# Attention in a whole-network kernel: the side chains placed one link per unit, the output bias as a product, x normalised on ScalarE, and a later wait for the last key stores

## The chip, the cores and the metric

The kernel is one program on one core of a Trainium2 chip. It computes the whole two-layer network in one launch. The metric is device time in microseconds; the kernel before ran in 1357.28 us (median of three runs, 1355.54 to 1359.51).

## The reference, cut to what matters

Eight batches of 256 rows by 512 pass through a long convolution, a quantised feed-forward layer, a cross attention with 16 heads of 32, and a mixture of experts. The change lies in the cross attention. The context has 256 rows and all of them count as image rows, so the image keys and values are all there is:

```python
q = rms_norm(layer_norm(x) @ Wq + bq, gq)     # per batch: 256 x 512
k = rms_norm(context @ Wk_img + bk_img, gk_img)
v = context @ Wv_img + bv_img
x = x + softmax(q k^T / sqrt(32)) v @ Wo + bo
```

float32 accuracy is kept by splitting a factor into two bf16 parts, high and low, and adding three products of them.

## The kernel before, in words

The stages run one after the other, each between barriers of all engines. `stage_keys_values` makes the keys and values of all batches and the queries of batches 0 and 1; keys go to DRAM in stacked form (`keys_stacked`), by three DMAs for each batch. Its SyncE program ends with waits for all its stores, the last batch's too, and the barrier waits for SyncE.

`stage_attention` walks 64 units, g = 8b + u: batch b, and u one of eight pairs of heads. Every engine has its own program, a Python loop over the same `STEPS` (b, u), written out by hand; an engine does its instructions strictly in that order and waits on semaphores. In a step, TensorE does: the transposed scores of unit g (L1551, waits for the maxima rows of g), the plain scores of g+2 (L1515, waits for the reduction of g+1), the turn of the maxima of g+1 (L1524), and the values of g-2 (L1537). VectorE copies the turned maxima into the queries' spare rows (L1449), reduces the scores of g+2 (L1467), and divides the output of g-2 (L1475, L1477). GpSimd splits the maxima of g+2 in two (L1368, L1370) and makes the low part of the probabilities of g (L1376). ScalarE does the exponential (L1422) and the high part (L1426). "The ring" in what follows is turn, copy, reduction, split, turn, which closes once for each unit.

Beside the units two side chains run, in extra instructions at fixed steps. Both use the two PSUM tiles `psP`.

- The query chain of batch b+2 (b+2 from 2 to 7): at u=4 VectorE normalises x into `xn` (L1498), at u=5 TensorE turns it (L1585), at u=6 the high part (ScalarE, L1413) and the low part (VectorE, L1461) are made and half of the 48 products done (`queries`, L1563 to L1568), the rest at u=7. At u=0 of the next batch ScalarE squares the last parts, GpSimd folds the squares (`fold_halves`, L915, L917), TensorE sums them (L908), VectorE makes v (L1482), GpSimd r = v^-1/2 (L1373); at u=1 ScalarE spreads r on diagonals (L1397), TensorE turns that into a row (L1594), VectorE scales the queries (four of L1486); at u=2 they are split (L1404, L1471) and from u=3 SyncE stacks them by 12 DMAs (L1336), which the plain scores of the batch after wait for.
- The output chain of batch b-1: at u=2 TensorE turns the output (L1601), at u=3 ScalarE and VectorE split it (L1408, L1455), and at u=3 and u=4 TensorE projects one tile each with 12 products (L893). VectorE adds the result to x (L1443) and takes statistics (L1492). The bias was added to x by GpSimd (`bias`, L1346).

So a step may hold a whole chain of four engines, with TensorE in the middle and at the end of it. At (0, 2) VectorE also clears the spare rows of the second key buffer (L1435, L1437).

## Time and profile before

| what | us |
|---|---|
| median of three runs | 1357.28 |
| profiled execution | 1357.12 |
| its span, first to last instruction | 1355.4 |
| attention stage, first instruction to the next stage's first | 593.1 to 890.8 |
| TensorE busy over the span | 1093.0 (81%) |
| VectorE / ScalarE / GpSimd busy | 930.0 / 712.1 / 618.7 |

A profile row of the windows view gives each engine's busy time in a stretch, with the count of its instructions in brackets, and then the granted TensorE clock as a share of 2.4 GHz (0.50 is 1.2 GHz). Matmuls overlap, so the time one takes on TensorE is read from the distance of two starts, and not from its duration.

### The profile page before, as it was taken

How to read it: one execution, taken by the hardware profiler on the slowest of the kernel's cores; microseconds unless marked ns; L12 is line 12 of the kernel's file. 1: busy time of each engine (PE TensorE's matmuls, PEld its weight loads, DVE VectorE, ACT ScalarE, POOL GpSimd, SP SyncE). 2: the span in 40 equal slices, each digit the busy share in tenths (PEclk: the TensorE clock that was granted, in tenths of full speed). 3: DMA queues.
4: the chain of work that ended last, by engine and by line, in shares of the span. 5: the costliest groups of instructions: out<-in, count | busy, mean ns of one | idle time of the engine just before them, and what ended most of it. 6: DMA issues, size and time to landing. Idle time of an engine off the chain costs nothing. (4 is left out here: it accounts for less than half of the span.)

```text
span 1355.4 us, 25553 instructions
## 1 busy us (share of the span) xinstructions
PE 1093.0 (81%) x9603; PEld 807.8 (60%) x9603; DVE 930.0 (69%) x1672; ACT 712.1 (53%) x1087; POOL 618.7 (46%) x580
## 2 busy tenths in 40 slices
PE   4899996369996699837888878788989879999950
PEld 4677775135553466515666655568756568888840
DVE  6489998858886676547787877678855545555526
ACT  4566755168885455425666666556424424454430
POOL 1444434224553222237776776630565335555520
PEclk9899998789999799858998998765989989999985
DMA  6574411003333313220111111067567747887749
GB/s 252 183 239 120 158 47 40 31 32 125 116 101 114 112 60 95 66 68 25 48 48 48 41 32 47 2 230 289 143 196 222 236 132 266 300 278 242 234 147 365
DMA packets 79291, 187.38 MB, mean 138 GB/s; under 512 B 10302, under 2 KB 12500, under 8 KB 78280
## 3 DMA queue, kind: packets, MB, share of 16 engines
q1 hardware_dynamic: 60040, 137.03, 30.3%
q0 software_dynamic: 8544, 24.68, 6.0%
q10 hardware_dynamic: 10592, 24.12, 5.7%
q8 instruction: 74, 1.21, 0.4%
q14 instruction: 41, 0.34, 0.1%
HBM read 131.37 MB, written 48.14 MB: 132 GB/s over the span
## 5 line engine op out<-in xcount | busy, mean ns | idle before, releaser
L376 PE MATMUL ps_y<-kv,toep 128*128 128x288 f32 x640 | 157.9, 409 | 6.9 <-DMA toep<-taps_padded 6.8
L376 PEld LDWEIGHTS ps_y<-kv,toep 128*128 128x128 f32 x640 | 122.0, 191 | 42.3 <-DMA toep<-taps_padded 8.3
L1376 POOL TENSOR_TENSOR at_pl<-at_pf,at_ph 128x1024 bf16<-128x1024 f32 x64 | 136.5, 2133 | 0.5 <-ACT at_ph L1426 0.5
L360 POOL TENSOR_TENSOR kv<-kx 128x1024 f32<-128x1024 f32 x32 | 60.6, 1894 | 88.9 <-PE ps_y L376 37.5
L1422 ACT ACTIVATE at_pf<-ps_st 128x1024 f32<-128x1024 f32 x64 | 65.3, 1020 | 59.2 <-PE ps_st L1551 55.1
L2205 POOL DMA_INDIRECT expert_results<-sgu,target x47 | 70.0, 1489 | 55.9 <-ACT sgu L2237 55.9
L1467 DVE TENSOR_REDUCE at_negmax<-ps_s 128x4 f32<-128x1024 f32 x64 | 78.2, 1222 | 14.4 <-PE ps_s L1515 12.8
L893 PEld LDWEIGHTS ps_eg<-e_xT,e_w 128*128 128x128 bf16 x1128 | 69.0, 100 | 14.3 <-DVE e_w L2278 1.9
L893 PE MATMUL ps_eg<-e_xT,e_w 128*128 128x128 bf16 x1128 | 73.1, 223 | 3.4 <-DVE e_xT L2285 3.4
L834 PE MATMUL ps_fH<-w1T,f_qaT 128*128 128x512 bf16 x256 | 64.6, 410 | 9.1 <-ACT f_h L742 8.4
L2278 DVE COPY e_w<-expert_weights 128x4096 bf16 x47 | 57.7, 1227 | 20.7 <-issue 20.7
L893 PE MATMUL ps_eu<-e_xT,e_w 128*128 128x128 bf16 x1128 | 71.2, 220 | 0.0
L1449 DVE COPY qs<-ps_m 32x256 bf16<-32x256 bf16 x128 | 37.6, 294 | 48.8 <-PE ps_m L1524 46.2
L1426 ACT ACTIVATE at_ph<-at_pf 128x1024 bf16<-128x1024 f32 x64 | 67.6, 1057 | 2.0
L2200 POOL DMA_INDIRECT sgu<-token_rows,token x45 | 44.4, 986 | 48.3 <-PE ps_ex L2327 48.3
L2291 DVE SCALAR_TENSOR_TENSOR e_y<-ps_eu,e_bias,e_y 128x128 f32<-128x128 f32 x94 | 28.7, 346 | 54.0 <-PE ps_eu L893 53.2
L893 PEld LDWEIGHTS ps_eu<-e_xT,e_w 128*128 128x128 bf16 x1128 | 65.6, 98 | 0.0
L1927 POOL TENSOR_TENSOR expert_weights<-s_raw,expert_weights 128x1024 bf16<-128x1024 f32 x16 | 37.6, 2351 | 53.3 <-ACT expert_weights L2084 53.2
L2253 ACT ACTIVATE e_xT<-ps_ex 128x512 bf16<-128x512 bf16 x47 | 28.1, 597 | 61.9 <-PE ps_ex L2327 61.9
L400 DVE TENSOR_TENSOR prod<-ps_y,qx 128x1024 f32<-128x1024 f32 x32 | 39.1, 1223 | 30.3 <-ACT ps_y L329 30.2
L859 PE MATMUL ps_fY<-w2T,f_qbT 128*128 128x512 bf16 x256 | 57.9, 379 | 0.8 <-DVE x_res L704 0.8
L2084 ACT ACTIVATE expert_weights<-s_raw 128x1024 bf16<-128x1024 f32 x32 | 33.7, 1054 | 45.7 <-DMA s_raw<-in_L_ffn_rg 34.6
(385 smaller groups left out, 3216.0 us busy)
## 6 DMA issues: line engine op xcount, KB each, us to landing
sgu<-down_parts SPq DMA_DIRECT2D x47, 512.0 KB, 4.8
w_raw<-in_L_ffn_w ACTq DMA_DIRECT2D x32, 512.0 KB, 5.1
toep<-taps_padded SPq DMA_DIRECT2D x32, 256.0 KB, 3.6
f_draw<-in_L_ffn_rw SPq DMA_DIRECT2D x16, 512.0 KB, 4.2
down_parts<-f_dparts SPq DMA_DIRECT2D x16, 512.0 KB, 2.9
s_raw<-in_L_ffn_rg SPq DMA_DIRECT2D x16, 512.0 KB, 4.4
s_raw<-in_L_ffn_rw SPq DMA_DIRECT2D x16, 512.0 KB, 5.4
m_got<-expert_results SPq DMA_DIRECT2D x16, 512.0 KB, 10.1
```

What stands on the lines that cost most here:

```text
L360: pool.tensor_tensor(pairs[:, :, :, 0:HD0], x[:, :, 0:HD0].unsqueeze(2).broadcast_to([P, ROWS_N, WIDE, HD0]), partners(x, 0, 1, WIDE), ALU ...
L376: last = pe.matmul(y[:, l * B:(l + 1) * B, :, WIDE - 1:], toep[h % 2][:, (DC - 1 - l + m) * P:(DC - l + m) * P], kv[h % 2][:, m * B:(m + 1 ...
L834: pe.matmul(psH[:, f, :], qaT[p][:, c, :], k.w1T[:, c * FF + f * 512:c * FF + (f + 1) * 512], start=(c == 0), stop=False)
L859: last = pe.matmul(psY[:, :], qbT[p][:, c, :], k.w2T[:, c * D:(c + 1) * D], start=(c == 0), stop=(c == FC - 1))
L893: instruction = pe.matmul(out, stationary[a], moving[b], start=first and n == 0, stop=last and n == 2)
L1376: pool.tensor_tensor(pl[u % 4][:, :, :, :], pf[u % 2][:, :, :, :], ph[u % 4][:, :, :, :], ALU.subtract) .then_inc(p_low, 1)
L1422: act.activation(pf[u % 2][:, :, :, :], psT[:, :, :, :], ACT.Exp, scale=SCORE_SCALE).then_inc(exped, 1)
L1426: act.activation(ph[u % 4][:, :, :, :], pf[u % 2][:, :, :, :], ACT.Copy).then_inc(p_high, 1)
L1467: dve.tensor_reduce(negmax[u % 2][:, :].rearrange("p (j q) -> p j q", j=2), psS[:, :, :, :], AX.X, ALU.max, negate=True).then_inc(max_read, 1)
L2200: pool.indirect_dma_start(out=rows[j % 2], out_offset=None, in_=k.scratch["rows"], in_offset=bass.IndirectOffsetOnAxis(ap=token[:, j:j + 1 ...
L2205: pool.indirect_dma_start(out=k.scratch["results"], out_offset=bass.IndirectOffsetOnAxis(ap=target[:, j:j + 1], axis=0), in_=yo[j % 2], in ...
L2278: dve.tensor_copy(w1[j % 2][:, :, :, :].rearrange("p h c f -> p (h c f)"), W[:, bass.ds(e, 1), :, :, :].rearrange("p o h c f -> p (o h c f ...
```

## The change

The two side chains are laid out anew, so that a step holds one link of a chain and the next link comes in a later step.

- Query chain of b+2: x is normalised by ScalarE at u=1 (`x_shift` = -mean*rstd as bias, rstd as scale); TensorE turns tile 0 at u=2 and tile 1 at u=3; products at u=4, 5, 6 (16 each); the eight square sums are eight products straight from the squares at u=7 (no fold), into the bank of the maxima (`psV`); VectorE's v and GpSimd's r and diagonals follow at u=7; TensorE's row and VectorE's scaling at u=0 of the next batch; the high part on ScalarE and the low part on GpSimd at u=2.
- Output chain of batch c: turned at (c+1, 7), split at the step after (ScalarE) and at the end of the same step (VectorE), projected in four halves at (c+2, 0) to (c+2, 3). For c=6 it is turned at (7, 4) and projected at (7, 5) and (7, 6); c=7 stays where it was.
- The output bias is the first product of each projected tile: a 33-row bf16 tile holds its high part in row 0 and its low part in row 32, against ones.
- The second wait of SyncE for the last batch's three key stores moves from the end of `stage_keys_values` to the load of batch 7's keys; the split keys' buffers live until then. The loads of keys and the stacking stand one or two steps earlier in SyncE's program.

```diff
+        self.last_stored = ctx.enter_context(nc.semaphore("last_keys_stored"))
...
+                done = k.last_stored if i == N - 1 else stacked[p]
...
-                sp.wait_ge(stacked[p], stores(N - 2 + p))
+                sp.wait_ge(stacked[p], stores(N - 2 - p))
...
+        bo = sb("at_bo", [LO_ROW + 1, D], F32)
+        bo_parts, ones_b = (sb(f"at_{n}", [LO_ROW + 1, w], BF16) for n, w in (("bop", D), ("oneb", P)))
+        x_shift = sb("at_xshift", [P, NT], F32)
...
+        maxes_and_sums = ctx.enter_context(nc.psum_tensor("ps_m", [P, D], F32))
+        psM = maxes_and_sums[:, 0:P].bitcast(BF16).rearrange("p (q t) -> p q t", q=2)
+        psV = maxes_and_sums[:, 2 * P:2 * P + TPB]
...
+        def turn_step(c):
+            return (c + 1, 7) if c < B - 2 else (B - 1, 4) if c == B - 2 else (B, 2)
+        def project_step(c, t, h):
+            return (c + 2, 2 * t + h) if c < B - 2 else (B - 1, 5 + t) if c == B - 2 else (B, 3 + t)
+        def following(step):
+            return step[0] + (step[1] + 1) // G, (step[1] + 1) % G
...
+            sp.wait_ge(bias_zeroed, 1)
+            for row in (0, LO_ROW):
+                sp.dma_start(bo[row:row + 1, :], k.ins["L1_xattn_bo"].rearrange("(o d) -> o d", o=1)).then_inc(b_loaded, 16)
...
-                if u == 2 and 0 < q < B:
+                if u == 0 and 0 < q < B:
                     if q >= 2:
                         sp.wait_ge(st_psum, (q - 1) * G)
-                    sp.dma_start(kb[q % 2][0:STACK, :, :, :], ks[q:q + 1, :, :, :, :].rearrange("o p h c s -> (o p) h c s"))                      .then_inc(k_loaded, 16)
-                if u == 3 and queried(q):
+                    if q == B - 1:
+                        sp.wait_ge(k.last_stored, KEY_INCS)
+                    sp.dma_start(kb[q % 2][0:STACK, :, :, :], ks[q:q + 1, :, :, :, :].rearrange("o p h c s -> (o p) h c s"))\
+                      .then_inc(k_loaded, 16)
+                if u == 2 and queried(q):
...
+            pool.memset(bo[:, :], 0.0).then_inc(bias_zeroed, 1)
+            pool.memset(ones_b[:, :], 1.0)
...
-                if b == 0 and u < AHEAD * TPB:
-                    pool.wait_ge(b_loaded, 16)
-                    bias(u)
-                if u == 5 and queried(b + 2):
-                    for t in range(TPB):
-                        pool.wait_ge(xn_ready, nth(b + 2) * TPB + t + 1)
-                        bias((b + 2) * TPB + t)
-                if u == 0 and queried(b + 1):
-                    q = nth(b + 1)
-                    pool.wait_ge(squared, (q + 1) * 2 * DC)
-                    fold_halves(pool, folded, 2 * q + 2, sq)
...
+                if u == 7 and queried(b + 2):
+                    n = nth(b + 2)
+                    pool.wait_ge(var_ready, n + 1)
+                    if n:
+                        pool.wait_ge(r_psum, n)
                     pool.tensor_tensor(r[:, :], v[:, :], k.pow_half[:, 0:TPB], ALU.pow).then_inc(r_ready, 1)
+                    pool.wait_ge(r_ready, n + 1)
+                    for t in range(TPB):
+                        last = pool.tensor_tensor(diag[:, t, :], k.ident[:, :], r[:, t:t + 1].broadcast_to([P, P]), ALU.mult)
+                    last.then_inc(diag_ready, 1)
...
+                if u == 2 and queried(b + 1):
+                    pool.wait_ge(q_high, nth(b + 1) + 1)
+                    pool.tensor_tensor(q_lo[:, :, :], qn[:, :, :], q_hi[:, :, :], ALU.subtract).then_inc(q_low, 1)
...
+                    act.wait_ge(q_low, q)
...
+                for c in range(B):
+                    if (b, u) == following(turn_step(c)):
+                        for t in range(TPB):
+                            act.wait_ge(ot_psum, c * TPB + t + 1)
+                            act.activation(o_hi[:, :, t * P:(t + 1) * P], psP[t][:, :].rearrange("p (c t) -> p c t", c=DC),
+                                           ACT.Copy).then_inc(ot_high, 1)
+                if u == 1 and queried(b + 2):
+                    act.wait_ge(shift_ready, 1)
                     for t in range(TPB):
...
+                        tile = (b + 2) * TPB + t
+                        act.activation(xn[t][:, :], xtile(tile), ACT.Identity, bias=x_shift[:, tile:tile + 1],
+                                       scale=x_rstd[:, tile:tile + 1]).then_inc(xn_ready, 1)
...
+                if u in (3, 4) and queried(b + 2):
+                    x_highs(nth(b + 2), u - 3)
+                if u in (5, 6) and queried(b + 2):
+                    biased_and_squared(nth(b + 2), u - 5)
                 if u == 7 and queried(b + 2):
...
+                    biased_and_squared(nth(b + 2), 2)
+                    biased_and_squared(nth(b + 2), 3)
...
+            dve.scalar_tensor_tensor(x_shift[:, :], x_mean[:, :], -1.0, x_rstd[:, :], ALU.mult, ALU.mult).then_inc(shift_ready, 1)
...
+                    lo_row = slice(LO_ROW, LO_ROW + 1)
+                    dve.wait_ge(b_loaded, 32)
+                    dve.tensor_copy(bo_parts[:, :], bo[:, :]).then_inc(bias_high, 1)
+                    dve.wait_ge(bias_high, 1)
+                    dve.tensor_tensor(bo_parts[lo_row, :], bo[lo_row, :], bo_parts[lo_row, :], ALU.subtract).then_inc(bias_low, 1)
...
+                if u == 7 and queried(b + 2):
+                    dve.wait_ge(sum_psum, nth(b + 2) + 1)
+                    dve.tensor_scalar(v[:, :], psV, 1.0 / D, RMS_EPS, ALU.mult, ALU.add).then_inc(var_ready, 1)
                 if u == 0 and queried(b + 1):
...
                     dve.wait_ge(r_psum, nth(b + 1) + 1)
                     for c in range(DC):
                         dve.scalar_tensor_tensor(qn[:, c, :], qn[:, c, :], vectors[:, ROWS["gq"] + c:ROWS["gq"] + c + 1],
...
+                                                 psP[1][:, 0:S], ALU.mult, ALU.mult).then_inc(normed, 1)
+                for c in range(B):
+                    if (b, u) == turn_step(c):
+                        out_lows(c)
                     for t in range(TPB):
...
+                        if (b, u) == following(project_step(c, t, 1)):
+                            statistics(c * TPB + t)
+                        if (b, u) == project_step(c, t, 1):
+                            added(c * TPB + t)
+                if u in (2, 3) and queried(b + 2):
+                    x_lows(nth(b + 2), u - 2)
...
+                if u == 1 and queried(b + 1):
+                    pe.wait_ge(var_ready, nth(b + 1) + 1)
...
+            def turn_x(b, q, t):
+                pe.wait_ge(xn_ready, q * TPB + t + 1)
+                if t:
                     pe.wait_ge(x_low, q * TPB + 1)
...
+                elif b >= 2:
+                    pe.wait_ge(y_added, (b - 2) * TPB + 1)
+                for c in range(DC):
+                    last = pe.transpose(psP[0][:, c * P:(c + 1) * P], xn[t][:, c * P:(c + 1) * P], k.ident[:, :])
+                last.then_inc(xt_psum, 1)
+            def query_highs(c, chunks):
+                cols = slice(c * P, (c + 1) * P)
+                for kc in chunks:
+                    pe.matmul(psP[c % 2][:, 0:S], qw[:, 0, kc, cols], x_hi[:, kc, :], start=(kc == 0), stop=False)
+                    pe.matmul(psP[c % 2][:, 0:S], qw[:, 1, kc, cols], x_hi[:, kc, :], start=False, stop=False)
+            def query_lows(c):
                 cols = slice(c * P, (c + 1) * P)
                 for kc in range(DC):
...
+                    last = pe.matmul(psP[c % 2][:, 0:S], qw[:, 0, kc, cols], x_lo[:, kc, :], start=False, stop=(kc == DC - 1))
                 last.then_inc(q_psum, 1)
+            def query_sums(g, q):
+                pe.wait_ge(squared, (q + 1) * 2 * DC)
+                pe.wait_ge(maxT_ready, 2 * (g + 2))
+                for t in range(TPB):
+                    for c in range(DC):
+                        last = pe.matmul(psV[:, t:t + 1], sq[:, c, t * P:(t + 1) * P], k.ones[:, 0:1], start=(c == 0), stop=(c == DC - 1))
+                last.then_inc(sum_psum, 1)
+            def spread(b, q):
+                pe.wait_ge(diag_ready, q + 1)
+                if b >= 2:
+                    pe.wait_ge(ot_low, (b - 1) * TPB)
+                pe.matmul(psP[1][:, 0:S], k.ones[:, :], diag[:, :, :].rearrange("p t q -> p (t q)"), start=True, stop=True)\
+                  .then_inc(r_psum, 1)
+            def turn_out(c):
+                pe.wait_ge(o_read, (c + 1) * G)
+                if c:
+                    pe.wait_ge(y_added, c * TPB)
+                if queried(c + 3):
+                    pe.wait_ge(squared, (nth(c + 3) + 1) * 2 * DC)
+                for t in range(TPB):
+                    for d in range(DC):
+                        last = pe.transpose(psP[t][:, d * P:(d + 1) * P], o[c % 2][:, t, d * P:(d + 1) * P], k.ident[:, :])
+                    last.then_inc(ot_psum, 1)
+            def project(c, t, h):
+                if h == 0:
+                    pe.wait_ge(ot_low, c * TPB + t + 1)
+                    if c == 0:
+                        pe.wait_ge(bias_low, 1)
+                    if t and queried(c + 3):
+                        pe.wait_ge(normed, (nth(c + 3) + 1) * DC)
+                    pe.matmul(psP[t][:, :], ones_b[:, :], bo_parts[:, :], start=True, stop=False)
+                for d in (2 * h, 2 * h + 1):
+                    last = three_products(pe, psP[t][:, :], [a[:, d, t * P:(t + 1) * P] for a in (o_hi, o_lo)],
+                                          [ow[:, s, d, :] for s in range(2)], False, d == DC - 1)
+                if h:
+                    last.then_inc(y_psum, 1)
             for b, u in STEPS:
                 g = b * G + u
...
                     scores(g + 2)
                 if unit(g + 1):
                     turn_maxes(g + 1)
...
                 if unit(g - 2):
                     values(g - 2)
+                if u in (2, 3) and queried(b + 2):
+                    turn_x(b, nth(b + 2), u - 2)
+                for c in range(B):
+                    if (b, u) == turn_step(c):
+                        turn_out(c)
+                    for t in range(TPB):
+                        for h in range(2):
+                            if (b, u) == project_step(c, t, h):
+                                project(c, t, h)
                 if u == 0 and queried(b + 1):
...
+                    spread(b, nth(b + 1))
+                if u == 4 and queried(b + 2):
+                    q = nth(b + 2)
+                    pe.wait_ge(x_low, q * TPB + 2)
+                    query_highs(0, range(DC))
+                    query_lows(0)
+                    if b >= 2:
+                        pe.wait_ge(y_added, (b - 1) * TPB)
+                    elif q:
+                        pe.wait_ge(normed, q * DC)
+                    query_highs(1, range(2))
+                if u == 5 and queried(b + 2):
+                    query_highs(1, range(2, DC))
+                    query_lows(1)
+                    pe.wait_ge(squared, nth(b + 2) * 2 * DC + 2)
+                    query_highs(2, range(DC))
                 if u == 6 and queried(b + 2):
...
+                    query_lows(2)
+                    pe.wait_ge(squared, nth(b + 2) * 2 * DC + 4)
+                    query_highs(3, range(DC))
+                    query_lows(3)
                 if u == 7 and queried(b + 2):
...
+                    query_sums(g, nth(b + 2))
```

## Rows read from the trace of the kernel before

**Rows 1.** Windows by batch: length, busy PE, PEld, DVE, ACT, POOL, clock, DMA share, GB/s

```profile
593.10:598.50 5.40, 3.32 (x14) 1.43 (x14) 2.86 (x4) 1.28 (x1) 0.99 (x4) 0.50 0.67 174
598.50:636.10 37.60, 25.79 (x287) 18.83 (x287) 26.20 (x43) 20.88 (x27) 27.39 (x32) 0.72 0.09 25
636.10:671.50 35.40, 28.94 (x368) 22.39 (x367) 27.63 (x56) 23.23 (x32) 26.30 (x30) 0.95 0.18 47
671.50:817.40 145.90, 119.15 (x1467) 90.71 (x1465) 110.56 (x224) 93.07 (x125) 105.08 (x117) 0.93 0.18 45
817.40:848.40 31.00, 24.30 (x307) 16.66 (x305) 23.68 (x50) 18.93 (x22) 21.59 (x25) 0.89 0.11 27
848.40:873.40 25.00, 21.47 (x268) 15.15 (x269) 18.47 (x43) 15.65 (x16) 17.59 (x22) 0.84 0.01 2
873.40:890.80 17.40, 11.77 (x104) 6.55 (x104) 5.57 (x12) 3.27 (x4) 4.09 (x2) 0.65 0.00 1
```

**Rows 2.** Waits of TensorE in the attention: total us, times, longest

```profile
PE ps_p L908 <- POOL at_sq L917: 11.0, 6, 1.8
...
PE ps_p L893 <- DVE at_olo L1455: 6.3, 8, 0.8
PE ps_p L1563 <- DVE at_xlo L1461: 6.0, 6, 1.0
PE ps_st L1551 <- ACT at_pf L1422: 5.8, 7, 0.9
```

**Rows 3.** Timeline of TensorE, one step: start, us, line and product

```profile
702.90 0.60 PE L1551 MATMUL ps_st<-qs,kb 128*128 128x256 bf16 x4
...
703.89 0.20 PE L1537 MATMUL ps_o<-v_hi,at_ph 128*128 128x33 bf16 x2
...
704.49 0.27 PE L1563 MATMUL ps_p<-at_xhi,qw 128*128 128x256 bf16 x1
...
707.11 0.60 PE L1551 MATMUL ps_st<-qs,at_kb 128*128 128x256 bf16 x4
```

**Rows 4.** Timeline of TensorE: the square sums of one batch and what follows

```profile
638.74 0.60 PE L908 MATMUL ps_p<-ones,at_sq 128*128 128x1 f32 x4 [1.84 <-POOL at_sq L917]
639.21 0.60 PE L1551 MATMUL ps_st<-qs,at_kb 128*128 128x256 bf16 x4
```

**Rows 5.** Timeline of TensorE: the projection of one tile and what follows

```profile
727.74 0.59 PE L893 MATMUL ps_p<-ow,at_ohi 128*128 128x512 bf16 x2
...
730.33 0.60 PE L1551 MATMUL ps_st<-qs,at_kb 128*128 128x256 bf16 x4
```

**Rows 6.** Timeline of GpSimd, two units with little beside them

```profile
846.18 2.13 POOL L1376 TENSOR_TENSOR at_pl<-at_pf,at_ph 128x1024 bf16<-128x1024 f32 x1
...
849.02 2.13 POOL L1376 TENSOR_TENSOR at_pl<-at_pf,at_ph 128x1024 bf16<-128x1024 f32 x1
```

**Rows 7.** One line, the normalising of x: ns least/median/most, first and last start

```profile
L1498 DVE TENSOR_SCALAR at_xn<-x_res,x_mean,x_rstd x12: 532/1268/2344, 620.6 to 804.1; 128x512 f32<-128x512 f32 x12
```

**Rows 8.** Timeline of all engines around the stage's start

```profile
582.47 0.62 SPq L1003 DMA_DIRECT2D keys_stacked<-kv_khi  x1
...
593.15 1.01 PE L1515 MATMUL ps_s<-kb,qs 96*128 96x256 bf16 x4 [16.08 <-PEq L931]
```

**Rows 9.** Waits of SyncE's queue around the stage's start

```profile
SPq L1040 <- DMA keys_stacked<-kv_khi: 9.5, 1, 9.5
```

**Rows 10.** Groups of instructions in the attention: busy us, mean ns

```profile
L1346 POOL TENSOR_TENSOR x_res<-x_res,at_bo 128x512 f32<-128x512 f32 x16 | 21.4, 1352 | 1.8 <-DVE at_xn L1498 1.8
...
L1601 PE MATMUL ps_p<-ident,at_o 128*128 128x128 f32 x64 | 10.3, 314 | 2.5 <-DVE at_qn L1486 1.9 <-DVE at_o L1477 0.6
L1486 DVE SCALAR_TENSOR_TENSOR at_qn<-at_qn,vectors,ps_p 128x256 f32<-128x256 f32 x24 | 9.9, 473 | 0.0
...
L1471 DVE TENSOR_TENSOR at_qlo<-at_qn,at_qhi 128x1024 bf16<-128x1024 f32 x6 | 7.3, 1216 | 0.0
...
L1594 PE MATMUL ps_p<-at_diag,ones 128*128 128x256 f32 x12 | 6.7, 659 | 0.1
```

More of the change, by code:

```diff
@@ L1613, in _ @@
                 if u == 7 and queried(b + 2):
-                    queries(nth(b + 2), 2)
-                    queries(nth(b + 2), 3)
+                    query_sums(g, nth(b + 2))
 E_N = 16
@@ L2445, in build @@
                 kb = left(attention, "kb0", [P, HC, DC, S], BF16)
+                k_hi, k_lo = ([left(attention, f"kv_{n}{i}", [P, DC, S], BF16) for i in range(2)] for n in ("khi", "klo"))
                 with ExitStack() as kv:
```

148 lines of the change are left out of this document (33 added, 115 removed).

## The prediction

> **What bounds the kernel now.** I read the windows by batch first. From 598.5 us to 873.4 us the 64 units take 274.9 us, and in the four middle batches (145.9 us, 36.5 each) TensorE is busy 119.15, so 29.8 of 36.5; VectorE 27.6, GpSimd 26.3, ScalarE 23.3 [rows 1]. No engine is full. Then the waits of TensorE: 11.0 us in six times for the folded squares, 6.3 for the low part of the output, 6.0 for the low part of x, 5.8 for the exponential [rows 2]: each is the tail of a side chain whose links stand in one step. Then TensorE's timeline, for what a step costs it when nothing waits: 1.59 us for a bare unit (702.90 to 704.49) and 2.62 for 24 query products, 0.109 each [rows 3]; 2.59 for the 12 products of a projected tile, 0.216 each [rows 5]; 0.47 for two float32 sums, 0.235 each [rows 4]. The ring of a unit with little beside it closes in 2.84 us (846.18 to 849.02) [rows 6]; no step can be shorter. Last, the stage's start: SyncE issues the last store at 582.47 to 583.09, then waits 9.5 us for it, and the stage begins at 593.1 [rows 8, 9].
>
> TensorE's work in a middle batch is now 8 x 1.59 = 12.7, 48 x 0.109 = 5.2 and 24 x 0.216 = 5.2, the turns 10.3 / 64 = 0.16 each, 16 of them 2.6, the row of r 6.7 / 6 = 1.1, the sums 0.5: 27.3 us [rows 3 to 5, 10]. So 9.2 us of each 36.5 is waiting, the ends of the last matmul before each wait included.
>
> **The change, part by part.** Added to TensorE in each batch with a query chain: eight sums in place of two, 6 x 0.235 = 1.4 us, and two bias products, 2 x 0.216 = 0.4. Work 29.1 us. By steps, the 1.59 of the unit in each:
> - u=0: bias product and half a tile 0.2 + 1.3, row of r 1.1: 4.2
> - u=1: half a tile 1.3: 2.9
> - u=2: turns 0.65, bias and half a tile 1.5: 3.75
> - u=3: turns and half a tile: 3.5
> - u=4, 5, 6: 16 products, 1.74: 3.33 each, 10.0
> - u=7: turns of the output 1.3, sums 1.9: 4.8
>
> All but u=1 lie well above the ring's 2.84 [rows 6], so TensorE sets the pace wherever its inputs are in time. I walked the other engines through these steps. Two places are late. At u=7 GpSimd stands from its split until the sums are in (the end of the step), then makes r and two diagonals, and only then the probabilities' low part, 2.13 [rows 6]; it is free again about 4.2 us into u=0, and the next split comes at 4.7, just when TensorE asks for it at u=1. VectorE meanwhile has four scalings, 4 x 0.473 = 1.9 [rows 10], after the row of r at the end of u=0, so the reduction that u=2 needs ends about 0.7 us late. At u=2 GpSimd takes the queries' low part behind its own work: the same form as the probabilities' low part, so 2.13 [rows 6] in place of 1.216 on VectorE [rows 10]; it pushes the split that u=4 waits for some 0.8 us past TensorE. Elsewhere (x's low part for u=3, the output's low part for u=0, the squares for the turns at u=7) my walk finds each input up to a microsecond early. So a middle batch is 29.1 + 0.7 + 0.8 = 30.6 us against 36.5: 5.9 saved, four times, 23.6.
>
> The diagonals on GpSimd are in no row. They cost something between nothing and the 1.35 of the bias addition, which has four times the elements [rows 10]; a quarter of it and a fixed part, 0.45 each, is what I took. With 1.35 each, GpSimd is 1.8 us later at u=1, all of it on the path.
>
> Off other engines: VectorE loses the normalising, two instructions of 1.27 us median (the least is 0.53), and the low part of the queries; GpSimd loses two bias additions, 2.7, and the folds, and gets 2.13 and the diagonals; ScalarE gets two normalisings for the diagonals and has 13 us idle in each batch [rows 1, 7, 10]. None of these is a term of its own: they are why the other engines keep up.
>
> The Trainium skill (SBUF — State Buffer, "Who interferes with whom") says that a VectorE instruction in a two-port mode and a GpSimd one exclude each other, and the second to issue waits for the whole of the first. The spread from 532 to 2344 ns agrees with it [rows 7]. Against the change speaks the GPSIMD Engine Reference, "Elementwise — side-by-side cycle accounting": a subtraction on GpSimd takes 1.96 times VectorE's time, which would make 2.38 of the 1.216; the trace has 2.13 for the form, a ratio of 1.75. By the page's factor the sum would be 1.5 us more over six batches.
>
> The other batches, by the same steps:
> - Batch 0, 37.6 now. It holds a step in which VectorE clears key rows and the ring stands; that stays, and two small bias instructions are added behind it, 1.2 us. The x chain is shorter by its waits in u=5 to u=7, some 4.5. Half clock stays at its start [rows 1]. 34.3.
> - Batch 1, 35.4 now: no projection; the row of r and GpSimd's block at u=1 (1.1 us exposed, for TensorE has less to do), the split at u=4. 29.0.
> - Batch 6, 31.0 now: no x chain, four halves of a projection, the scaling. Steps at the ring, those of u=0, 2 and 4 about a microsecond above. 26.5.
> - Batch 7 to the last exponential, 25.0 now: two steps with a whole tile at 1.59 + 2.8 = 4.4, five near the ring, 3.0: 23.9, say 24.0.
>
> Sum 34.3 + 29.0 + 4 x 30.6 + 26.5 + 24.0 = 236.2 against 274.9: 38.7 saved. The end of the stage (17.4 us) [rows 1] keeps its chain and gets two bias products: 0.4 lost.
>
> **The start.** The wait for the last store goes, 9.5 us [rows 9]. What is late next: SyncE's own third issue, to 583.09 [rows 8]; its wait for the other buffer's stores, issued a whole item earlier, is over by then. The DMAs of the stores now run beside the first units, and batch 1's keys and the bias queue behind them, but batch 1's keys are wanted some 30 us later. Lost again: two memsets on GpSimd ahead of the first split, which my bounds put between 0 and 1.35 (an instruction with as many elements a partition, [rows 10]); I take 0.7. Net 8.8. The moved loads and stacking in SyncE's program wait on the same semaphores as before, in the same order, so their place alone is worth nothing.
>
> **Sum.** The profiled execution took 1357.1 us, 0.2 below the median of 1357.28 and 1.7 above its span. 1357.1 - 38.7 + 0.4 - 8.8 = 1310.0.
>
> **The rivals.**
> - The chains lie apart, but TensorE stays as it is in rows: its busy time of 29.8 a batch contains the ends of matmuls and the stretches at 1.2 GHz (granted 0.93) [rows 1]. If none of that goes, a batch is 29.8 + 1.8 + 1.5 = 33.1; in batches 1 to 5 that is 2.5 more each, 12.5 in all: 1322.5. For it: GpSimd and VectorE both have steps above the ring, and each new wait leaves a matmul's end bare. Against: most of those ends stand before waits that go. Dear diagonals (0.9 each above my price, 1.8 in six batches, 10.8) come out at the same place.
> - No wait is left at all: 29.1 a batch, 1.5 less in six, 9.0: 1301.0. For it: inputs are late by less than a microsecond. Against: GpSimd's block at u=7 is plain in the order.
> - The start isn't gained, because entry into the stage waits for something else (the other buffer's stores, instructions not yet there): 1310.0 + 8.8 = 1318.8. For it: all engines stood idle there and no row shows what else was ready.
> - Slower: the queries' low part, now on GpSimd behind its units, comes late to SyncE's stacking, and the plain scores for the next batch (first wanted in u=6) stand for it. By my walk GpSimd ends its split for u=3 at 8.3 us into the batch, the low part of unit 1 at 10.4, the next split at 11.3 (the reduction is late), the low part of unit 2 at 13.4 and the queries' at 15.6; the last DMAs I put 5 later (no row here), 20.9; the steps up to u=5 and the two waits add up to 22.5, when the scores are asked: 1.6 us of slack. Beyond that each microsecond counts in full, in six batches; from 1.6 + (47.1 / 6 = 7.9) = 9.5 us late it eats the whole gain, and at 10.5 late the kernel takes 1363. For it: seven instructions of GpSimd stand ahead of it. Against: none of them waits for long.
>
> **How the numbers follow.** Forecast 0.5, busy TensorE or dear diagonals 0.25, no waits 0.1, no gain at the start 0.09, late stacking 0.06 (of which 0.04 as far as slower, and 0.02 at no change). I predict 1310 us. The range 1297 to 1332 takes in the first three rivals, with both bounds of the diagonals and memsets, and leaves out late stacking and sums of several mishaps. A measurement of this kernel tells about 0.3%, 4 us, from no change; so faster 0.94, same 0.02, slower 0.04.
>
> **What would show it.** The windows by batch: 30 to 31 us in the middle ones, TensorE busy over nine tenths. The waits view: none for folded squares, none of TensorE for x's low part; what remains are waits for GpSimd's split of the maxima at u=1 and u=4, and for the reduction at u=2. At the start the first scores at about 583.6. On TensorE the eight sums in 1.9 us. If batches take 33 us with a clock below 0.95, the first rival holds; if the plain scores wait for the stacking, the last. I am wrong if a wait that I found early by a microsecond is late, for these repeat in every batch.

## The result and the profile after

The changed kernel ran in 1311.38 us (median of four runs, 1302.65 to 1321.37), the kernel before beside it in 1357.94: a ratio of 0.966 [0.958, 0.975]. The four runs lie 1.4% apart, more than those of the kernel before; the profiled one was the slowest, 1321.37. I profiled the same kernel a second time (first experiment below); that execution took 1308.49. Both stand here, for the gap between them is a finding of its own: of its 12.9 us, 2.8 lie before the attention, 6.9 in it and 3.2 behind it.

| stretch, us | before | forecast | after, first profile | after, second profile |
|---|---|---|---|---|
| up to the attention stage | 593.1 | 583.6 | 586.2 | 583.4 |
| attention stage | 297.7 | 260.1 | 262.7 | 255.8 |
| from there to the end | 466.3 | 466.3 | 472.5 | 469.3 |
| profiled execution | 1357.1 | 1310.0 | 1321.4 | 1308.5 |

The last stretch is what is left of the execution's time. The first profile by the same windows as [rows 1]: the entry, batches 0, 1, 2 to 5, 6, 7 up to the last exponential, and the tail (columns as there).

```profile
586.20:591.70 5.50, 3.40 (x14) 1.45 (x14) 3.09 (x5) 1.28 (x2) 1.59 (x6) 0.50 0.57 194
591.70:625.60 33.90, 25.84 (x298) 20.61 (x299) 24.63 (x44) 22.20 (x28) 18.83 (x26) 0.75 0.13 34
625.60:656.20 30.60, 26.23 (x356) 21.66 (x355) 20.75 (x48) 24.09 (x31) 23.23 (x29) 0.90 0.24 58
656.20:777.30 121.10, 118.98 (x1522) 93.18 (x1521) 96.86 (x213) 96.07 (x124) 94.00 (x113) 0.96 0.22 54
777.30:806.60 29.30, 25.89 (x311) 17.89 (x310) 23.07 (x51) 18.59 (x20) 23.65 (x29) 0.83 0.12 29
806.60:830.80 24.20, 24.03 (x304) 16.10 (x302) 20.31 (x45) 15.46 (x18) 18.69 (x20) 1.00 0.01 3
830.80:848.90 18.10, 12.19 (x103) 6.18 (x99) 6.38 (x14) 3.23 (x4) 2.25 (x2) 0.81 0.00 0
```

The four middle batches take 121.1 us where they took 145.9, and TensorE is busy 98% of it instead of 82%: its own work sets the pace, as the experiment that takes six products away shows again below. The second profile, the same windows from batch 2 on:

```profile
653.40:769.60 116.20, 112.80 (x1514) 91.36 (x1521) 96.92 (x213) 96.00 (x124) 94.03 (x113) 1.00 0.23 56
769.60:796.90 27.30, 23.05 (x309) 16.70 (x310) 23.15 (x51) 18.61 (x20) 23.76 (x29) 0.94 0.13 32
796.90:821.00 24.10, 23.41 (x296) 16.02 (x299) 20.17 (x44) 15.39 (x17) 18.53 (x20) 1.00 0.01 3
```

The instructions are the same; the granted clock is 1.00 where the first profile has 0.96, and the batches take 29.0 each, where the first profile has 29.0 for the first of the four and 30.7 for the other three. Waits of the attention in the first profile (total us, times, longest), to be read against [rows 2]:

```profile
PE ps_st L1579 <- DVE qs L1491: 9.0, 6, 5.6
...
PE ps_s L1540 <- DVE at_negmax L1497: 7.0, 16, 1.3
...
PE ps_m L1552 <- POOL at_maxes L1377: 3.7, 6, 1.7
...
PE ps_o L1565 <- POOL at_pl L1390: 2.4, 1, 2.4
...
PE ps_p L1638 <- DVE at_olo L1458: 0.6, 1, 0.6
```

The folded squares, the low part of x and the exponential are gone from TensorE's waits, and of 6.3 us for the output's low part 0.6 is left. What remains is almost all the units' own ring, and 5.6 of the 9.0 us is one wait in batch 0, at the step in which VectorE clears key rows.

The stage's start, against [rows 8, 9] (start, us, engine and line):

```profile
584.82 0.62 SPq L1004 DMA_DIRECT2D keys_stacked<-kv_khi  x1
586.19 0.56 POOL L1360 MEMSET at_maxes<- 128x256 bf16 x2 [4.30 <-POOLq L933]
...
586.23 1.01 PE L1540 MATMUL ps_s<-kb,qs 96*128 96x256 bf16 x4 [6.81 <-PEq L933]
...
586.69 0.52 POOL L1361 MEMSET at_bo<- 33x512 f32 x1
587.16 0.20 POOL L1362 MEMSET at_oneb<- 33x128 bf16 x1
```

From the end of the last issue (585.44) to the first scores 0.8 us pass, where it was 10.1. The two new memsets take 0.7, but the first split of the maxima comes 2.8 us after the start, as it did before (2.7): the reduction is later than they are.

### The profile page after: what moved, and what is told of

It is laid out like the page before. It is cut to its first block and busy times, and to the rows that moved or that the text cites. A ratio compares the mean times of both kernels' runs of the same rounds, so it can differ in the third digit from the quotient of the medians.

```text
span 1319.6 us, 25710 instructions
## 1 busy us (share of the span) xinstructions
PE 1101.8 (83%) x9691; PEld 816.9 (62%) x9691; DVE 908.2 (69%) x1657; ACT 716.9 (54%) x1087; POOL 595.9 (45%) x572
## 5 line engine op out<-in xcount | busy, mean ns | idle before, releaser
L1491 DVE COPY qs<-ps_m 32x256 bf16<-32x256 bf16 x128 | 37.6, 294 | 35.2 <-PE ps_m L1552 32.1
L401 DVE TENSOR_TENSOR prod<-ps_y,qx 128x1024 f32<-128x1024 f32 x32 | 39.1, 1223 | 30.8 <-ACT ps_y L330 30.7
## 6 DMA issues: line engine op xcount, KB each, us to landing
m_got<-expert_results SPq DMA_DIRECT2D x16, 512.0 KB, 10.1
```

## The experiments

Times are medians beside the kernel before on the same chip; the gap is against that one. A batch's length is read between the first exponentials of two batches, and a step's in the same way. The stretches of each profiled execution:

| kernel, us | up to the attention | attention | from there to the end | profiled |
|---|---|---|---|---|
| the same again | 583.4 | 255.8 | 469.3 | 1308.5 |
| later wait alone | 581.8 | 298.2 | 471.8 | 1351.8 |
| attention without the later wait | 594.4 | 253.6 | 469.9 | 1317.9 |
| queries' low part on VectorE | 583.5 | 253.7 | 472.5 | 1309.7 |
| one square product | 585.4 | 248.4 | 473.5 | 1307.3 |
| whole tiles | 585.5 | 275.7 | 469.9 | 1331.0 |
| bias on GpSimd | 583.1 | 260.1 | 476.2 | 1319.4 |
| x normalised on VectorE | 583.9 | 266.4 | 473.3 | 1323.6 |
| later wait alone, additions later | 585.8 | 300.3 | 472.8 | 1358.8 |
| rows cleared early | 580.7 | 250.2 | 472.9 | 1303.8 |
| and statistics later | 585.1 | 255.8 | 472.4 | 1313.3 |

The program behind the attention is the same in all of them, and it took from 469.3 to 476.2 us. So a gap of a few microseconds between two medians does not yet tell what an edit did in the attention; the third column is read beside it. Each is one execution.

### The same kernel again

No edit.

> The changed kernel as it is, for its own spread: four runs gave 1302.7, 1304.7, 1318.0 and 1321.4, and the one trace so far is of the longest. Theory A (clock): in that trace each of batches 3 to 6 has one stretch at 1.2 GHz right after the eight square sums, and its first step takes 5.4 us where batch 2, without the stretch, has 3.7; batches are 30.7 with and 29.0 without. Then a trace of a 1303 run shows middle batches of 29.0 and an attention some 7 to 10 us shorter. Theory B (elsewhere): middle batches are 30.7 in every trace and the spread lies in other stages, the mixture of experts above all, which was 4.4 + 1.7 us longer in that trace than in the one of before. Times either 1303 to 1305 or 1318 to 1321.

Measured: 1309.0 us (1308.5 to 1320.2), ratio 0.963 [0.958, 0.968]. The middle batches are 29.0 us each, as theory A had it, and the attention is 6.9 us shorter, at the lower edge of its 7 to 10; the other 6.0 us of the gap lie outside, which is theory B's part. Three of the four times fall between the two groups that the theory named. Inside the attention the clock's level is what differs. TensorE at the end of batch 4 and in step u=0 of batch 5, first profile:

```profile
744.28 1.84 PE L1610 MATMUL ps_m<-ones,at_sq 128*128 128x1 f32 x16
745.99 0.60 PE L1579 MATMUL ps_st<-qs,at_kb 128*128 128x256 bf16 x4
...
748.11 1.03 PE L895 MATMUL ps_p<-ow,at_ohi 128*128 128x512 bf16 x2
748.94 0.63 PE L895 MATMUL ps_p<-ow,at_olo 128*128 128x512 bf16 x1
749.37 1.06 PE L895 MATMUL ps_p<-ow,at_ohi 128*128 128x512 bf16 x2
750.22 0.63 PE L895 MATMUL ps_p<-ow,at_olo 128*128 128x512 bf16 x1
```

and the same place in the second:

```profile
738.24 1.84 PE L1610 MATMUL ps_m<-ones,at_sq 128*128 128x1 f32 x16
739.94 0.60 PE L1579 MATMUL ps_st<-qs,at_kb 128*128 128x256 bf16 x4
...
742.38 0.38 PE L895 MATMUL ps_p<-ow,at_olo 128*128 128x512 bf16 x1
742.59 0.59 PE L895 MATMUL ps_p<-ow,at_ohi 128*128 128x512 bf16 x2
743.02 0.38 PE L895 MATMUL ps_p<-ow,at_olo 128*128 128x512 bf16 x1
```

(Each of the eight sums stands as two records, hence x16.) The two products with the low part start 0.64 apart at full clock (742.38 to 743.02) and 1.28 apart at half (748.94 to 750.22). The step takes 5.4 us in place of 3.7. Its window in the first profile (u=0 of batch 5), and then the eight steps of batch 4 in the second, whose first row is the same step without the stretch:

```profile
746.60:752.00 5.40, 5.40 (x45) 3.22 (x44) 3.55 (x9) 3.50 (x5) 5.24 (x7) 0.68 0.03 6
```

```profile
711.50:715.30 3.80, 3.64 (x45) 2.67 (x45) 3.59 (x9) 3.53 (x5) 3.64 (x6) 1.00 0.04 13
715.30:718.20 2.90, 2.83 (x40) 1.74 (x37) 2.81 (x7) 2.87 (x3) 2.17 (x2) 1.00 0.01 3
718.20:722.60 4.40, 4.00 (x46) 2.71 (x48) 4.24 (x11) 2.69 (x5) 3.65 (x6) 1.00 0.32 75
722.60:726.00 3.40, 3.40 (x47) 2.58 (x46) 2.98 (x7) 2.60 (x4) 3.40 (x2) 1.00 0.28 63
726.00:729.70 3.70, 3.48 (x52) 2.95 (x50) 3.51 (x8) 2.89 (x5) 3.28 (x7) 1.00 0.30 71
729.70:733.00 3.30, 3.30 (x52) 3.02 (x50) 2.28 (x6) 2.83 (x4) 2.46 (x4) 1.00 0.02 5
733.00:736.70 3.70, 3.70 (x56) 3.38 (x55) 2.20 (x5) 3.57 (x7) 2.85 (x4) 1.00 0.00 0
736.70:740.60 3.90, 3.90 (x58) 3.82 (x57) 2.68 (x7) 3.04 (x6) 2.10 (x4) 1.00 0.81 202
```

The second block is to be held against the list of steps in the prediction. TensorE has full steps at u=3, 5, 6 and 7 and is short of a few tenths in the others. The stretch at 1.2 GHz costs 1.7 us in three of four middle batches of the first profile, and the lowered clock in batch 6 costs 3.3 (29.3; 26.0 in a later kernel whose batch 6 is at clock 1.00).

### The later wait alone

```diff
  (the kernel before, with these lines of the change)
+                done = k.last_stored if i == N - 1 else stacked[p]
...
-                sp.wait_ge(stacked[p], stores(N - 2 + p))
+                sp.wait_ge(stacked[p], stores(N - 2 - p))
...
+                    if q == B - 1:
+                        sp.wait_ge(k.last_stored, KEY_INCS)
```

> The kernel before with the later wait for the last key stores alone. Theory A: the entry into the attention no longer stands for the stores; in the trace of the whole change the stage began 0.75 us after the last issue in place of 10.0. No memsets are added here, so the time falls by 9.3, from 1357.5 to about 1348. Rival: the stores, now beside the first units, hold up something else (the load of batch 1's keys behind them), and half or less is kept: 1353 or more.

Measured: 1355.6 us (1351.8 to 1360.3), ratio 0.995 [0.993, 0.997]: 7 us gained where the entry alone is worth over 9. Batch 0 takes 40.5 us in place of 37.6, and step u=1 of it 6.1 in place of 3.2. GpSimd's waits at the stage's start:

```profile
POOL x_res L1348 <- DMA at_bo<-in_L_xattn_bo: 4.6, 1, 4.6
```

That is the bias spread over 128 rows, 256 KB. It landed 4.7 us after its issue in the kernel before and takes 10.7 here, now that it follows the last stores on SyncE's queue; the additions of the bias stand ahead of GpSimd's next split. The changed kernel loads two rows of the bias, which VectorE first reads at 604.9 in its first profile, 17 us after their issue, and so loses nothing here.

### The attention without the later wait

```diff
-                done = k.last_stored if i == N - 1 else stacked[p]
+                done = stacked[p]
...
-                sp.wait_ge(stacked[p], stores(N - 2 - p))
+                sp.wait_ge(stacked[p], stores(N - 2 + p))
...
-                    if q == B - 1:
-                        sp.wait_ge(k.last_stored, KEY_INCS)
```

> The whole change but the later wait. Theory A: the terms add, so this is the changed kernel plus 9.3: 1312 to 1314 in its shorter runs, 1327 to 1330 in its longer ones; the attention from first to last exponential stays at 239 us. Rival: with the wait back, the units begin with all stores landed and the loss is smaller, 5 or less.

Measured: 1320.9 us (1317.9 to 1322.9), ratio 0.969 [0.966, 0.972], 11.8 above the whole change where 9.3 were expected. In the profiles the stage begins 11.0 later than in the second one of the change. The middle batches are 29.0 each, and SyncE's wait is back as in [rows 9]:

```profile
SPq L1041 <- DMA keys_stacked<-kv_khi: 9.5, 1, 9.5
```

So the two parts are worth 41 us and 7 us alone; together 53. Of the 5 us between, 2.9 are the longer batch 0 of the experiment before, which the whole change doesn't have; the rest I can't place. Batch 1 takes 29.0 here and not 30.6: its u=4 is at clock 1.00 and takes 5.3 (7.1).

### The queries' low part back on VectorE

```diff
-                    pool.tensor_tensor(q_lo[:, :, :], qn[:, :, :], q_hi[:, :, :], ALU.subtract).then_inc(q_low, 1)
+                    dve.tensor_tensor(q_lo[:, :, :], qn[:, :, :], q_hi[:, :, :], ALU.subtract).then_inc(q_low, 1)
```

> The changed kernel with the low part of the queries back on VectorE at u=2 (1.22 us there, 2.13 on GpSimd). Theory A (my prediction's step): GpSimd's 2.13 at u=2 pushes the split that u=4 needs past TensorE; in the trace TensorE waits 0.2 in middle batches and 1.7 in batch 1. Gone, that is 0.2 to 0.4 in each of five batches and 1.7 once: 2 to 4 us faster than the changed kernel, within its spread; the waits of TensorE for the split (3.7 us in 6) fall below 2. Rival (the reason for the move): VectorE is the tighter of the two at u=2, the reductions come later by 1.2 and TensorE waits for them: 1.2 in each of six batches, 5 to 8 us slower.

Measured: 1310.5 us (1309.4 to 1313.0), ratio 0.962 [0.959, 0.965]: no difference in the time, where 2 to 4 us less were expected. The attention alone is 2.1 shorter in the profile, too little to be seen beside what the rest of the kernel varies. In a middle batch u=3 becomes 4.0 (3.4) and u=4 becomes 3.4 (3.7), 29.4 in all (29.0); batch 1 becomes 28.4 (30.6), its u=4 falling from 7.1 to 4.1. The placement moves a delay from one engine's queue to the other's.

### One square product for each tile in place of four

```diff
-                    for c in range(DC):
-                        last = pe.matmul(psV[:, t:t + 1], sq[:, c, t * P:(t + 1) * P], ...
+                    last = pe.matmul(psV[:, t:t + 1], sq[:, 0, t * P:(t + 1) * P], k.ones[:, 0:1], start=True, stop=True)
```

Three quarters of the squares are left out of the sum.

> The changed kernel with two square sums in place of eight at u=7 (three quarters of the squares are left out of the norm of the queries). Theory A: the sums are on TensorE's path, 0.235 us each, so 6 x 0.235 = 1.4 in each of six batches, 8.5 us faster than the changed kernel run beside it, middle batches 27.6 in place of 29.0; and the stretch at 1.2 GHz that followed the sums in one trace doesn't come, so the spread over runs shrinks. Rival: u=7 and u=0 are set by GpSimd (r, diagonals, low part), which starts earlier by the same 1.4, but VectorE and the split at u=1 hold the pace: half of it, 4 us. A third: without the sums TensorE idles instead and the clock falls more often: no gain.

Measured: 1308.3 us (1307.3 to 1308.5), ratio 0.962 [0.960, 0.963]. A middle batch is 28.0: u=7 falls by 0.9, u=0 by 0.3, and u=1 rises by 0.1. Six products cost 1.0 us and not the 1.4 of the sum of rows; at their measured price, 0.214 each, they are 1.3, and TensorE stands 1.0 us of such a batch where it stood 0.5 of the 29.0, so part of what they took turns into waits. The median is less than 1 us below the change, though theory A had 8.5. The attention did get 7.4 shorter in the profile; the stretches before and behind it are 2.0 and 4.2 longer there than in the second profile of the change.

### Projection by whole tiles again

```diff
-            return (c + 2, 2 * t + h) if c < B - 2 else ...
+            return (c + 2, 2 * t) if c < B - 2 else ...
```

> The changed kernel with each projected tile done whole, at u=0 and u=2, in place of four halves at u=0 to 3. TensorE's work is the same. Theory A (spreading matters where a step falls to the ring's 2.84): u=0 and u=2 get 1.3 more each, u=1 falls only from 3.0 to 2.85 and u=3 from 3.4 to about 2.9, so 2.0 more in each of six batches, 12 us slower than the changed kernel. Rival: TensorE's sum of work sets the batch, and the other engines catch up in the long steps what they lacked in the short: 0 to 3 us.

Measured: 1331.9 us (1328.6 to 1334.3), ratio 0.979 [0.976, 0.982], 23 above the change, about twice what was expected. VectorE's additions to x and its statistics move along with the products. Two steps of batch 3, u=1 and u=2:

```profile
693.90:697.00 3.10, 1.70 (x34) 1.26 (x31) 3.01 (x8) 2.98 (x3) 0.87 (x1) 1.00 0.01 3
697.00:703.10 6.10, 5.30 (x52) 3.31 (x54) 4.20 (x10) 2.69 (x4) 4.95 (x6) 1.00 0.37 88
```

The step without a half of the projection does not get shorter by 1.3: it stays at 3.1, with TensorE busy 1.7, for it waits 1.4 for the ring's copy. The long steps pay in full, and only the one behind u=2 gives something back (2.5 for 3.4), since the ring ran on beside the products. So this batch is 32.0, 2.9 more, at clock 1.00. The other three middle batches take 33.1 to 33.5: there the clock falls in u=2, behind the step in which TensorE had little to do. Batch 2:

```profile
660.50:663.70 3.20, 1.77 (x34) 1.33 (x32) 3.11 (x8) 3.02 (x3) 0.94 (x1) 1.00 0.00 0
663.70:671.10 7.40, 6.45 (x52) 3.79 (x54) 4.16 (x10) 2.68 (x3) 6.26 (x7) 0.77 0.30 71
```

The attention is 19.9 us longer in the profile. Even filling of the steps is the largest single part of the gain found here.

### The bias on GpSimd again

```diff
+                if b == 0 and u >= 4:
...
+                    bias(u - 4)
+                if u == 5 and queried(b + 2):
+                    for t in range(TPB):
...
+                        bias((b + 2) * TPB + t)
...
-                    pe.matmul(psP[t][:, :], ones_b[:, :], bo_parts[:, :], start=True, stop=False)
```

> The changed kernel with the bias added to x by GpSimd again (two of 1.3 us at u=5, as before; the first four tiles at (0, 4) to (0, 7)) and no bias product. Theory A: TensorE is the pace and gains two products of 0.216 in each of eight batches, 3.5 us; but GpSimd has under 0.8 us idle at u=5 in the trace of the changed kernel, so its 2.6 make the split late and TensorE waits about 2 in each of six batches: 12. Net 8 us slower. Rival: low parts and splits catch up before anyone waits, and the kernel is 3 us faster than the changed one.

Measured: 1317.8 us (1316.2 to 1319.4), ratio 0.968 [0.966, 0.970]. GpSimd around step u=5 and 6 of batch 3:

```profile
704.92 2.13 POOL L1403 TENSOR_TENSOR at_pl<-at_pf,at_ph 128x1024 bf16<-128x1024 f32 x1
707.02 2.49 POOL L1370 TENSOR_TENSOR x_res<-x_res,at_bias 128x512 f32<-128x512 f32 x2
709.47 0.21 POOL L1388 TENSOR_TENSOR at_maxes<-at_negmax,ones 128x4 bf16<-128x4 f32 x1
```

The next split stands behind 2.49 us of additions, and u=6 takes 4.8 (3.6). The two bias products cost TensorE 0.4 a batch and take that away: the batch is 30.0 with the additions, 29.0 with the products. Batch 0 loses 4.4, 38.3 (34.0): three additions stand in one step there. Batches 1, 6 and the end of the stage are a little shorter, so the attention is 4.3 us longer in all; the stretch behind it is 6.9 longer in the profile, where nothing was edited. That the time came out near the expected 8 is in part luck.

### x normalised on VectorE again, in the new place

```diff
-                        act.activation(xn[t][:, :], xtile(tile), ACT.Identity, bias=x_shift[:, tile:tile + 1],
+                        dve.tensor_scalar(xn[t][:, :], xtile(tile), x_mean[:, tile:tile + 1], x_rstd[:, tile:tile + 1],
```

> The changed kernel with x normalised by VectorE again, two instructions at the end of u=1. Theory A: VectorE's two take 1.27 each beside GpSimd's subtraction and stand ahead of the copy and the reduction of u=2, which already are late (TensorE waits 0.8 in that step): 2 us more in each of six batches, 12 us slower. Rival: VectorE has the time, since it idles a microsecond in each of u=4 to 7, and what is late at u=2 is made up by u=4: 0 to 3 us slower; then the move to ScalarE was worth nothing.

Measured: 1322.9 us (1318.1 to 1324.7), ratio 0.971 [0.969, 0.974]. VectorE's instructions and TensorE's turn of x, and then the step u=2:

```profile
693.79 2.48 DVE L1522 TENSOR_SCALAR at_xn<-x_res,x_mean,x_rstd 128x512 f32<-128x512 f32 x2
695.86 0.66 PE L1591 MATMUL ps_p<-ident,at_xn 128*128 128x128 f32 x4 [1.47 <-DVE at_xn L1522]
696.29 0.62 DVE L1485 COPY qs<-ps_m 32x256 bf16<-32x256 bf16 x2
696.94 1.23 DVE L1491 TENSOR_REDUCE at_negmax<-ps_s 128x4 f32<-128x1024 f32 x1
```

```profile
692.70:698.70 6.00, 4.16 (x46) 2.77 (x48) 5.84 (x12) 2.66 (x4) 2.88 (x6) 1.00 0.37 86
```

The copy and the reduction of the ring stand behind 2.48 us. TensorE itself waits 1.5 of them for the normalised x that it turns in this step, and u=2 takes 6.0 (4.4). On ScalarE the two take 0.80 each and nobody waits. In the prediction this move was no term of its own; undone, it costs 2.4 us a batch at clock 1.00, and 2.9 in the two middle batches whose clock falls (0.95). How much of it is the ring and how much TensorE's own wait, this run doesn't part.

### Two trials on the start of the stage

Before with the later wait, and the bias additions moved from (0, 0..3) to (0, 4..7):

```diff
-                if b == 0 and u < AHEAD * TPB:
-                    bias(u)
+                if b == 0 and u >= AHEAD * TPB:
+                    bias(u - AHEAD * TPB)
```

> The kernel before with the later wait alone, as in start_only, and GpSimd's first four bias additions at (0, 4) to (0, 7) in place of (0, 0) to (0, 3). In start_only the bias's load (256 KB) stood behind the last stores, GpSimd waited 4.6 us for it at (0, 0) and the units stood with it: batch 0 took 40.5 us against 37.6, which is where 3 of the expected 9.3 went. Theory: moved, the load has landed before it is wanted, batch 0 is 37.6 again and the kernel is 9.3 us faster than the kernel before, ratio 0.993. Rival: GpSimd's additions at (0, 4) and (0, 5) meet the x chain of that batch there and cost what they saved: ratio 0.995 as in start_only.

Measured: 1357.3 us (1347.9 to 1360.9), ratio 0.996 [0.994, 0.997]. The theory fell: batch 0 takes 41.7 us, with 10.7 in its u=6, where the additions meet the query chain. The wait for the DMA is gone (u=1 is back at 3.2), but moving its user costs as much.

Then the whole change with the second key buffer's spare rows cleared by GpSimd in the stage of keys, so that VectorE's two memsets leave step (0, 2), and the two small bias instructions at (0, 6):

```diff
+            pool.memset(kb[1][STACK:, :, :, :], 0.0).then_inc(rows_zeroed, 1)
...
+            pool.memset(kb[1][STACK:STACK + 2, :, :, :], 1.0).then_inc(rows_zeroed, 1)
...
-                if b == 0 and u == 2:
-                    dve.memset(kb[1][STACK:, :, :, :], 0.0).then_inc(ones_set, 1)
...
-                    dve.memset(kb[1][STACK:STACK + 2, :, :, :], 1.0).then_inc(ones_set, 1)
```

> The changed kernel with the spare rows of the second key buffer set by GpSimd early in the stage of keys and values, where it has nothing else to do for 16 us, in place of VectorE at (0, 2), and the bias's two parts made at (0, 6). In the trace of the changed kernel the step (0, 2) takes 9.7 us where its neighbours take 3.0 to 3.8, and TensorE stands 5.6 for VectorE. Theory: the step falls to 3.4 and the kernel is 6 us faster than the changed one, about 0.958 of before. Rival: the units then run ahead of the load of batch 1's keys, which stands behind the last stores, and wait for it at the first plain scores of batch 1; or TensorE keeps 1.2 GHz longer: 2 to 3 us.

Measured: 1306.6 us (1303.7 to 1308.7), ratio 0.959 [0.957, 0.961], the lowest median of all, though its interval still meets that of the change (0.963 [0.958, 0.968]). Its batches 0, 1, and 2 to 5:

```profile
586.20:615.60 29.40, 25.66 (x297) 20.26 (x298) 21.33 (x42) 22.09 (x28) 19.20 (x26) 0.79 0.15 44
615.60:646.00 30.40, 26.76 (x357) 22.24 (x356) 20.79 (x48) 24.16 (x32) 23.19 (x29) 0.87 0.22 53
646.00:762.20 116.20, 114.05 (x1522) 91.36 (x1520) 96.90 (x213) 96.06 (x124) 94.17 (x113) 1.00 0.23 56
```

Step (0, 2) takes 3.9 in place of 9.7, and (0, 7) 5.6 in place of 3.7, at a mean clock of 0.81: batch 0 gains 4.5 of the 6 expected.

### The statistics later

On top of the last kernel:

```diff
+        def stats_step(c, t):
+            return (c + 2, 5 + t) if c < B - 2 else following(project_step(c, t, 1))
-                        if (b, u) == following(project_step(c, t, 1)):
+                        if (b, u) == stats_step(c, t):
```

> rows_cleared_early, and the statistics of the output rows (0.68 us each on VectorE, two in a batch) at u=5 and u=6 of the batch in place of u=2 and u=4. Nothing in the stage waits for them. Theory: VectorE is what u=2 and u=3 wait for (the reduction after the four scalings, then the low part of x), and it idles 0.8 to 1.0 in u=5 and u=6; so 0.3 to 0.6 less in each of six batches, 2 to 4 us faster than rows_cleared_early, middle batches 28.5. Rival: what TensorE waits for at u=2 lies ahead of the first statistics in VectorE's order, and the wait at u=4 is GpSimd's: middle batches stay at 29.0.

Measured: 1313.3 us (1311.8 to 1316.6), ratio 0.964 [0.962, 0.966], 6.7 above the kernel without this move. The middle batches are 29.0 and 29.1 at full clock and 30.7 in the two whose u=0 takes 5.4. The step u=2 stays at 4.4, so the statistics were not what TensorE waits for there. Of the 9.5 us between the two profiles 5.6 lie in the attention, and the stretches at 1.2 GHz, back in two middle batches and in batch 6, are more than that (1.7 twice and 3.5); 4.3 lie before it. Whether the move brings the stretches on or they came by chance, one profile can't tell.

## Why the prediction was right

The time, 1311.4 against 1310.0, and the mechanism both held: side chains apart, TensorE at its own pace. The terms were less exact than their sum, and that the sum lies within 1.4 us of the median is in part luck. In the second profile the attention is 4.3 us shorter than forecast and the stretch behind it 3.0 longer; in the first the attention is 2.6 longer and the stretch behind it 6.2.

- **Middle batches, forecast 30.6.** 29.0 to 30.7 in the first profile, 29.0 in the second. TensorE's work was put at 29.1, waits at 1.5. At full clock the steps came out at 3.7, 3.0, 4.4, 3.4, 3.7, 3.4, 3.6, 3.9, where the prediction had 4.2, 2.9, 4.45, 3.5, 4.1, 3.3, 3.3, 4.8. Too dear in it were u=0 and u=7: the row of r takes 0.43 between starts at full clock (1.1 in the sum, from busy times, which overlap and were partly taken at 1.2 GHz), the sums 1.7 (1.9), the turns 0.9 for eight (1.3, from busy times too). The wait at u=2 is there but half as long (TensorE waits 0.32 for the reduction, 0.7 in the sum); that at u=4 is 0.2 to 0.3 and not 0.8, except in batch 1. So the figure of 30.6 is met by a batch with a stretch at 1.2 GHz, which the prediction did not have, and not by the waits.
- **No step shorter than the ring's 2.84.** That reading of [rows 6] is too strong, though little in the sum hung on it. The kernel before has a step of 2.0 at (6, 5), behind one of 4.2, and the change with whole tiles has steps of 2.5 and 2.0 behind long ones. The ring bounds steps in a row; behind a long step, in which it ran on, one can be shorter.
- **The queries' low part on GpSimd, forecast 2.13.** 2.13. The Trainium skill (GPSIMD Engine Reference, "Elementwise — side-by-side cycle accounting") has the factor 1.96 from a float32 addition of 2048 elements. Carried over to this subtraction, 1.96 times VectorE's 1.216, it gives an estimate of 2.38; the measurement decides for the row.
- **Diagonals, forecast 0.45 each** between nothing and 1.35: 0.40. The rival of dear ones is out.
- **Batch 0, forecast 34.3**: 33.9. **Batch 7, 24.0**: 24.2.
- **Batch 1, forecast 29.0**: 30.6. Its u=4 takes 7.1: TensorE stands 1.7 for the split behind the queries' low part, and the clock falls in the step (0.77 over it). At clock 1.00, in the kernel without the later wait, it is 5.3, and batch 1 is the forecast 29.0; with the low part on VectorE it is 4.1. This is the wait that I had put in every batch; it is large only where TensorE has no projection to do and comes early.
- **Batch 6, forecast 26.5**: 29.3 and 27.2, 26.0 where the clock is full.
- **Tail, 0.4 lost**: 0.7 to 0.8.
- **Start, 9.5 gained, memsets 0.7**: from the last issue to the stage 9.3 gained, memsets 0.1 or less. In the first profile the stage of keys itself ended 2.3 us later than in that of before.
- **Nothing after the stage**: 3 to 6 us more from there to the end in the two profiles of the change, and 5.5 in that of the later wait alone, whose attention is that of before. In every profile but that of before this stretch is longer than 466.3 (469.3 to 476.2). What the difference is I didn't find; other chips may be part of it (the kernel before had medians of 1360 to 1363 on those of the experiments).

Of the rivals: "TensorE as it is in rows" named the stretches at 1.2 GHz as a cost that may stay, and that part of it is what the first profile has, at 1.7 a batch and not 2.5; the bare ends of matmuls that it kept did not stay. "No waits" is near the second profile in the middle batches (29.0), though not in the time: 1308.5 and not 1301.0. The start was gained. Late stacking did not occur: in batch 2 the last stacking DMAs are issued by 673.2 and land 2.0 us after their issue, where I had put 5; the first plain scores that need them come at 677.5, so the slack is over 2 us.

Not undone alone were the new places of the query chain and the square sums without the fold; for these only the waits speak, 11.0 us for the folded squares and 6.0 for the low part of x, which are gone from the list.

## What to carry to other kernels

When a ring of small dependent steps runs beside long side chains, steps in a row are no shorter than the ring, and a step emptied of side work gives little back; spread the extra work of the busiest engine evenly over the steps, and give each step one link of each chain: undoing the evenness cost 23 us here, over two fifths of the gain. Additions of 2.5 us that nobody waited for still cost 1.0 us a batch, because the next link of the ring stood behind them in their engine's order; look for an engine on which such work stands ahead of nothing. A wait that is taken away at a stage's end lets its DMAs run into the next stage: look at which load comes behind them on that queue, and who wants it first.

## What the hardware showed unexpectedly

- The same kernel runs with or without stretches at 1.2 GHz in the steps behind the eight one-column float32 sums, with TensorE busy before and in them (5.4 of 5.4 us). They cost 1.7 us a middle batch where they occur. The three long runs of this kernel (1318.0 to 1321.4 us) have a mean granted clock of 0.897, the five short ones (1302.7 to 1309.6) 0.905 to 0.911.
- That the sums bring the stretches on is not shown. With only two sums there were none in the middle batches and the runs lie within 1.2 us, but the second profile and six edited kernels with all eight sums have none behind the sums in middle batches either, and with whole tiles the clock fell elsewhere, behind a step in which TensorE was busy 1.8 of 3.2 us. Why the chip grants one run the full clock and not the next stays open.
- A load of 256 KB landed 10.7 us after its issue behind three stores on the same queue, against 4.7 with the stores over.
- One instruction, the normalising of 128x512 float32 on VectorE, took from 534 to 2355 ns in its new place too, its median 538, its mean 1182. On ScalarE the same work took 797 to 801 ns in all twelve.
